# Query normalisation and softmax maximum moved into sixteen ACT exponentials per tile

## What is computed

```python
qkv = x @ Wqkv                                  # 16 heads of 64
q = l2norm(q) * qs
k = l2norm(k) * ksc
q = q * cos * scale + rotate_half(q) * sin * scale
k = k * cos / scale + rotate_half(k) * sin / scale
sim = einsum(q, k) * 8.0                        # windows of 32 queries, 64 keys
sim = where(mask, -max, sim)
attn = softmax(sim, -1)
out = einsum(attn, v)
```

## Time and profile before

| what | value |
|---|---|
| median of 3 runs | 3847.91 us (3847.8 to 3848.5) |
| the profiled execution | 3848.15 us |
| its span, first to last instruction | 3846.4 us |
| TensorE busy | 3455.1 us, 90% |
| VectorE busy | 3085.4 us, 80% |
| GpSimd busy | 2917.2 us, 76% |
| ScalarE busy | 2349.1 us, 61% |

### The profile page before, as it was taken

One profiled execution on the slowest core, in us unless ns is written; L12 is line 12 of the kernel. 1 busy time (PEld: TensorE's weight loads), 2 busy tenths in 40 slices (PEclk: granted clock), 3 DMA queues, 4 the chain that ended last, 5 costly groups with the idle time before them and its releaser, 6 DMA issues. The chain is left out here.

```text
span 3846.4 us, 100641 instructions
## 1 busy us (share of the span) xinstructions
PE 3455.1 (90%) x40888; PEld 2309.6 (60%) x40888; DVE 3085.4 (80%) x5682; ACT 2349.1 (61%) x3523; POOL 2917.2 (76%) x1934
## 2 busy tenths in 40 slices
PE   3699999999999999996999689999999999999997
PEld 3466666666666666663777356666666666666664
DVE  2588888888888888883666588888888888888885
ACT  1466666666676676662333356666677666666663
POOL 0699989999999899971000399989999989899992
PEclk8799999999999999997999799999999999999998
DMA  5100000000000000001000000000000000000000
GB/s 180 64 2 2 2 29 2 29 2 2 29 2 2 29 2 2 2 2 70 1 1 1 1 2 2 2 29 2 2 29 2 2 29 2 29 2 2 2 2 12
DMA packets 31648, 58.66 MB, mean 15 GB/s; under 512 B 11350, under 2 KB 23766, under 8 KB 27350
## 3 DMA queue, kind: packets, MB, share of 16 engines
q1 hardware_dynamic: 31190, 52.23, 4.0%
HBM read 42.79 MB, written 9.44 MB: 14 GB/s over the span
## 5 line engine op out<-in xcount | busy, mean ns | idle before, releaser
L395 POOL TENSOR_TENSOR arena<-arena 128x512 f32<-128x512 f32 x768 | 960.4, 1273 | 146.3 <-ACT arena L746 91.2
L404 POOL TENSOR_TENSOR arena<-arena 128x1024 f32<-128x1024 f32 x384 | 907.6, 2364 | 30.1
L411 POOL TENSOR_TENSOR arena<-arena 128x1024 f32<-128x1024 f32 x384 | 723.0, 1904 | 207.1 <-DVE arena L512 207.0
L958 PE MATMUL ps_a<-w_qk,stream 128*128 128x512 f32 x1536 | 752.1, 613 | 30.9 <-DVE arena L522 27.2
L975 PE MATMUL ps_h<-arena,w_vo 128*128 128x256 f32 x3072 | 732.3, 381 | 0.0
L522 DVE TENSOR_TENSOR arena<-ps_a,arena 128x1024 f32<-128x1024 f32 x384 | 465.1, 1211 | 296.5 <-POOL arena L382 171.5
L975 PEld LDWEIGHTS ps_h<-arena,w_vo 128*128 128x128 f32 x3072 | 564.3, 191 | 66.6
L951 PEld LDWEIGHTS ps_t<-ident,arena 128*128 128x128 f32 x3072 | 355.8, 143 | 354.2 <-POOL arena L411 241.7
L951 PE MATMUL ps_t<-ident,arena 128*128 128x128 f32 x3072 | 410.5, 277 | 116.3 <-POOL arena L411 116.3
L528 DVE TENSOR_REDUCE arena<-arena 128x16 f32<-128x1024 f32 x384 | 455.6, 1208 | 3.2 <-ACT arena L794 0.2
L805 ACT ACTIVATE arena<-ps_a 128x1024 f32<-128x1024 f32 x192 | 196.6, 1024 | 422.0 <-PE ps_t L969 422.0
(11 more groups left out here) (143 smaller groups left out, 6078.2 us busy)
## 6 DMA issues: line engine op xcount, KB each, us to landing
w_qk<-fWqkv SPq DMA_DIRECT2D x12, 1024.0 KB, 4.9
w_vo<-vo_scr SPq DMA_DIRECT2D x10, 1024.0 KB, 7.4
vo_scr<-arena SPq DMA_DIRECT2D x4, 1024.0 KB, 4.0
w<-w_scr SPq DMA_DIRECT2D x10, 341.0 KB, 8.7
arena<-fWqkv SPq DMA_DIRECT2D x6, 512.0 KB, 7.3
arena<-fWo SPq DMA_DIRECT2D x6, 512.0 KB, 8.2
w<-fW SPq DMA_DIRECT2D x12, 192.0 KB, 5.7
rope<-c_rope SPq DMA_DIRECT2D x1, 2048.0 KB
```

The lines of the kernel that those rows point to most:

```text
L395: last = pool.tensor_tensor(dst[:, :, h, :], src[:, :, 1 - h, :], tab[:, h:h + 1, :].to_broadcast([P, HEADS, DH // 2]), ALU.mult)
L404: pool.tensor_tensor(r, r, swapped, ALU.add).then_inc(add_s, 1)
L411: pool.tensor_tensor(r, r, rn[st.par(LP)][:, n * HEADS:(n + 1) * HEADS].unsqueeze(2) .to_broadcast([P, HEADS, DH]), ALU.mult).then_inc(rot ...
L958: last = pe.matmul(A[:, n * 512:(n + 1) * 512], stream[:, c0:c0 + P], w_qk[:, st.layer(LP) % 2, off:off + 512], start=True, stop=True)
```

## The change

The exponent of a score s of a head with query factor r and unscaled maximum m is `r * (s - m)`. Before, the query was multiplied by r ahead of the scores and m was subtracted from the scores. After the change the query is transposed without its factor; VectorE computes `nmax = (smax * -1) * r` for the 16 heads in one small operation in place of the difference over 1024 columns; and ScalarE takes sixteen exponentials of 64 columns in place of one of 1024, each with the head's r as scale and nmax as bias, both read from SBUF, one number a partition. The key keeps its factor. TensorE's transposes of the query wait for GpSimd's sum (`add_q`) and no more for its product (`rot_q`). The buffer `nmax` and the semaphore `bias_done` are new, `rot_q` and `sub_done` go.

```diff
@@ GpSimd
                 if st.on(LP):
-                    normalise(0, add_q, rot_q)
                     normalise(1, add_k, rot_k)
@@ VectorE
                     dve.tensor_reduce(smax, s3, AX, ALU.max).then_inc(max_done, 1)
                     dve.wait_ge(max_done, st.count(LS))
-                    dve.tensor_tensor(s3, s3, smax.unsqueeze(2).to_broadcast([P, HEADS, SLOTS]), ALU.subtract)\
-                       .then_inc(sub_done, 1)
+                    dve.wait_ge(root_done, Step(st.s - 1, st.block).roots())
+                    scale = rn[st.par(LS)][:, 0:HEADS].rearrange("p (c e) -> p e c", e=2)
+                    dve.scalar_tensor_tensor(nmax.rearrange("p (e c) -> p e c", e=2),
+                                             smax.rearrange("p (e c) -> p e c", e=2), -1.0, scale,
+                                             ALU.mult, ALU.mult).then_inc(bias_done, 1)
@@ ScalarE
                 if st.on(LG):
-                    act.wait_ge(sub_done, st.count(LG))
-                    act.activation(S[:], S[:], ACT.Exp).then_inc(exp_done, 1)
+                    act.wait_ge(bias_done, st.count(LG))
+                    for h in range(HEADS):
+                        cols = slice(h * SLOTS, (h + 1) * SLOTS)
+                        n = 2 * (h % PAIRS) + h // PAIRS
+                        last = act.activation(S[:, cols], S[:, cols], ACT.Exp, bias=nmax[:, h:h + 1],
+                                              scale=rn[st.par(LG)][:, n:n + 1])
+                    last.then_inc(exp_done, 1)
@@ TensorE
                 if st.on(LS):
-                    pe.wait_ge(rot_q, st.count(LS))
+                    pe.wait_ge(add_q, st.count(LS))
                     wait(pe, mean_t, st.count(LG, 1))
```

More of the change, by code:

```diff
@@ L175, in build @@
         smax = carve(HEADS)
+        nmax = carve(HEADS)
         ssum = carve(HEADS)
@@ L251, in build @@
         (table_ready, proj_q, proj_k, raw_q, raw_k, sq_q, sq_k, t1_q, t1_k, red_q, red_k, sw_q, sw_k, add_q, add_k,
-         root_step, root_done, rot_q, rot_k) = map(
+         root_step, root_done, rot_k) = map(
             sem, ("table_ready proj_q proj_k raw_q raw_k sq_q sq_k t1_q t1_k red_q red_k sw_q sw_k add_q add_k "
-                  "root_step root_done rot_q rot_k").split())
-        (qt_ps, qt_sb, kt_ps, kt_sb, halo, scores_ps, max_done, sub_done, exp_done, sum_done, rsum_done, prob_done) = map(
-            sem, ("qt_ps qt_sb kt_ps kt_sb halo scores_ps max_done sub_done exp_done sum_done rsum_done "
+                  "root_step root_done rot_k").split())
+        (qt_ps, qt_sb, kt_ps, kt_sb, halo, scores_ps, max_done, bias_done, exp_done, sum_done, rsum_done, prob_done) = map(
+            sem, ("qt_ps qt_sb kt_ps kt_sb halo scores_ps max_done bias_done exp_done sum_done rsum_done "
                   "prob_done").split())
```

## The result

The changed kernel takes 4862.64 us (median of 4 runs, 4860.44 to 4869.55) where the kernel before takes 3848.20 (4 runs). The ratio is 1.2636 with a 95% interval from 1.262 to 1.2652: 1014 us slower.

What follows compares the result with a forecast made beforehand. Waiting chains, not one engine, were taken to bound the kernel: ScalarE and TensorE close one step of a pair, VectorE the other. 3848 + 831 (sixteen exponentials) + 380 (clock) = 5059 us; own range 4830 to 5270, wider range 4650 to 5280.

Steps and rivals of the forecast that it cites:

- (1): GpSimd's query product goes, 1.904 us, 192 times; counted as nothing, since another wait ends later.
- looser bound: GpSimd as third bound: its products wait 207.0 us for VectorE's root, TensorE's transposes 116.3 us for them.
- (2): VectorE's difference, 1.23 us a tile, becomes one 0.19 us operation; saves 1.04 us in B, nothing in A.
- B: Step without the FFN's hidden layer, 15.27 us before, closing through VectorE; forecast as T + 13.22.
- the tie that the prediction named: In B, TensorE's chain from L1037 to the next query copy also makes T + 13.2, equal to VectorE's.
- (3): One exponential becomes sixteen on ScalarE, 366 ns start to start, 5.86 us; 8.75 us more a pair, 831 us.
- Neighbours overlap: Rival: each small exponential starts 0.10 us before the last one's end, 266 ns apart, T = 4.26; chance 0.20.
- A: Step with the FFN's hidden layer, 17.87 us before, closing through ScalarE, TensorE and ScalarE; forecast as T + 16.95.
- T: Time of the sixteen exponentials on ScalarE, taken as 5.86 us; the pair of steps is 30.17 + 2T.
- (4): TensorE's clock halves for about 5 us after both gaps: 2.5 us lost in A, 1.5 in B, 380 us.
- The clock holds: Rival: the gaps come but TensorE's granted clock stays at 1.00, 4679 us; chance 0.10.
- The signs: Expected profile: 3072 exponentials, VectorE's largest wait for them, ScalarE's query-product wait shrinking or moving, TensorE gaps about 5 and 4 us.

Runs made afterwards that it cites:

- e2: Kernel before with sixteen exponentials reading a factor of 1 and a bias of 0 from memory; difference and query product stay: 4865.81 us, ratio 1.2643.
- e7: Kernel before with ScalarE's copies of the transposed query and xn_t ahead of the one exponential in steps with a hidden layer: 3851.07 us, ratio 0.9997.
- e6: Changed kernel with one exponential of 1024 columns and a constant scale; factor and maximum computed but not applied: 3740.34 us, ratio 0.9711.
- e1: Kernel before with its one exponential cut into sixteen of 64 columns, without factor and bias from memory: 4011.77 us, ratio 1.0427.
- e5: Changed kernel with the bias from memory but the factor as a constant (0.001): 4379.05 us, ratio 1.1372.
- e3: Changed kernel with seven idle-time products of 256 columns on TensorE in each of the two gaps of a pair of steps: 4484.92 us, ratio 1.1652.
- e8: Changed kernel with ScalarE's query and xn_t copies ahead of the exponentials, window-input transposes later on TensorE, their copy behind the second GELU: 4876.48 us, ratio 1.2665.

## Why the prediction was right, and where it was off

5059 us were forecast, 4863 came, inside the range and clearly slower. Point by point:

**(1) The query product brings nothing.** Right in the changed kernel: with it and the difference put back (e2) the time is the same. The reason given fits the rows: L542 waits for the exponentials (799.4 us) and L992 for the copy behind them. But "looser bound" was wrong for the kernel before. There the loop of VectorE and GpSimd was as long as the path I read from ScalarE's and TensorE's rows: e7 shortened that path, the pair stayed at 33.1 us, and the rows of the loop add up to just that. A row in which an engine starts when a copy ends shows that this was the last wait, not that no other path is just as long.

**(2) The difference saves 1.04 us in B.** With one exponential the removals are worth 109 us (e6), and the steady pair is 0.98 us shorter, all of it in B, near the 1.04 of the sum. But the sum gave all of this to the difference and nothing to the query product. The loop that e7 shows doesn't hold the difference, and with both products in it it takes 33.15 us, so without the product's removal the pair could hardly have become shorter. Neither removal was tried alone with one exponential. The small operation was put at 0.19 us and took 0.58 on average. Behind the sixteen B isn't closed by VectorE any more: 998.16 and 1042.54 follow a query copy that TensorE's queue released, as in the tie that the prediction named.

**(3) Sixteen exponentials in 5.86 us.** This is the term that was mis-sized: they take 4.64. The step that failed is "As the pair with a bias doesn't overlap, I take 366 ns from start to start too". They last longer than I took (418 ns) and overlap more (293 from start to start). The rival *Neighbours overlap* had the right mechanism, with 266 ns. The pair at L848, the row I held to be nearest in kind, misled: 32 partitions and 512 columns, and 0.68 us apart, where 428 + 54 + 90 would be 0.57. Why it didn't overlap wasn't tried. The price of an operand came out as 90 to 92 ns, not far from the 80 of the earlier trace rows. The Trainium skill gives 93 ns for it ("ScalarE: Activation LUTs", section What ACT_TABLE_LOAD costs), and e1, e5 and the changed kernel agree. The estimate of 332 ns from the same section's figures is above the 293 measured, since its base is higher: by them a plain instruction of 64 columns would start 146 ns after the one before, and e1 shows 111.

**The chains.** A = T + 16.95 and B = T + 13.22 hold where the clock stays at 1.00. The prediction used one T for two things: A counts the exponentials to the next start on ScalarE (4.64 us for the sixteen), B to their end (4.82 in the changed kernel). With these e3 should have A = 21.59 and B = 18.04; its exponentials at 1000.03, 1021.70 and 1039.79 give 21.67 and 18.09. e1 gives a second point, with 1.67 and 1.96 us and the difference still there (14.26 instead of 13.22): A = 18.62, B = 16.22. Measured are 18.82 (1004.40 to 1023.22) and 16.20 (to 1039.42).

**(4) The clock.** Both gaps cost a spell, as forecast: 6 us at 0.50 in A, 5.5 in B. L992, L966 and L959 lost (2.08 - 1.13) + (3.62 - 1.88) + (1.42 - 1.04 for the transposes at 1009.59) = 3.1 us in A. Against e3's steps A lost 3.0 us (24.66 - 21.67) and B 1.6 (19.72 - 18.09). That is 4.6 a pair instead of 4.0. That the whole kernels differ by 378 us, against 380 in the sum, is in part luck: 95 pairs at 4.6 would be 438, but in the first six steps of a block the changed kernel loses only some 3 us to e3 (114.2 and 111.5 us in the first block). The rival *The clock holds* is out.

**The sum.** T was 1.22 us too long in A (5.86 for 4.64) and 1.04 in B (for 4.82): 215 us too many. The clock's part was 0.6 a pair too little: 57 too few. e3's steps are 0.13 a pair longer than the chains give: 12 too few. 5059 - 215 + 57 + 12 = 4913. The remaining 50 us come from taking 95 equal pairs: the steps in which a block fills are shorter (the first exponentials start at 148.34, 167.86, 186.28 and 203.32, 17 to 19.5 us apart). The first six steps of a block grew by 16.1 us in the first block (98.1 to 114.2) and 15.6 in the second (100.0 to 115.6), where three steady pairs grow by 33.7; that is 36 of the 50.

**The signs.** Seen as told: 3072 exponentials, VectorE's largest wait now for them, TensorE's gaps before L992 and L959 (4.3 and 3.6 us, forecast 5 and 4), a clock of 0.858. ScalarE's wait for the query product didn't shrink: 349.9 us against 350.5.

## What to carry to other kernels

Before cutting one ACTIVATE into many so that each can take its own factor and bias, multiply the spacing of such instructions, 293 ns for 64 columns here against 54 ns of work in them, by their number, and ask who stands behind them in that engine's queue. A factor for each head and row was cheaper here as one VectorE multiplication of 1.23 us over all heads; and a softmax whose exponents are known to be bounded needs no maximum, which has to be shown from the gains too, not from the normalised vectors alone. An idle stretch that a change makes on TensorE can be paid twice, once as the gap and once as the 5 to 6 us at half clock behind it: so it was for gaps of 3.6 and 4.3 us here, not for those of up to 1.5 us in e3, and for a gap of 2.11 us once so and once not (e5). And before shortening the path that the rows show, look whether a second one is as long, as in e7.

## What was not expected of the hardware

The duration of a small ACTIVATE says little about its cost. Without operands it is 293 ns with the next one 111 ns later; with one 338 and 201; with two 418 and 293. Copies that follow look longer too: L754's 598 ns became L762's 696 without a change of that instruction.

The small operation on 128x16 that replaced the difference was taken at 0.19 us like L512. It took 175 to 922 ns, 583 on average:

```profile
1019.03 0.73 POOL L383 TENSOR_TENSOR arena<-rope,qk_gain 128x256 f32<-128x256 f32 x1
1019.07 0.71 DVE L590 SCALAR_TENSOR_TENSOR arena<-arena 128x16 f32<-128x16 f32 x1
...
1040.82 0.73 POOL L383 TENSOR_TENSOR arena<-rope,qk_gain 128x256 f32<-128x256 f32 x1
1040.97 0.61 DVE L590 SCALAR_TENSOR_TENSOR arena<-arena 128x16 f32<-128x16 f32 x1
```

Both times it ends 0.02 to 0.03 us after GpSimd's table product, begun just before it. In e8, at a moment when GpSimd is idle, the same operation takes 0.18 us (1023.48). L512, which it was likened to, reads PSUM. The Trainium skill says that a VectorE instruction with two SBUF inputs contends with a GpSimd instruction that reads SBUF ("SBUF — State Buffer", section Who interferes with whom). These rows agree with it. It was not tried by itself here, and it cost no time that counts, since ScalarE waited 6.7 us for this operation in the whole run.
